# Slot reduction of the edge features by halving adds instead of a strided reduce, in a four-layer graph network on one core

## The chip, the core and the metric

The kernel runs on one core of a Trainium2 chip. The metric is device time in microseconds of one execution. The program is one launch; nothing else runs on the core. Its engines are named as in the profile: PE (TensorE), DVE (VectorE), ACT (ScalarE), POOL (GpSimd) and SP (SyncE, which here only issues DMAs).

## The reference

Four graph layers stand one behind the other, each with a residual and a layer norm, over 3125 nodes of 64 channels and 100,000 edges sorted by destination. The change is in the second layer, whose aggregation is this:

```python
xi = ew * m[dst]; xj = ew * m[src]; ea = ew * (edge_attr[:, :3] @ We + be)
h = jnp.concatenate([xi, xj, ea], axis=-1) @ Wpre + bpre
s1 = segment_sum(h, dst);  s2 = segment_sum(h * h, dst)
mn = segment_min(h, dst);  mx = segment_max(h, dst)
```

So for each node and each channel four values are folded over the node's incoming edges: the sum of h, the sum of its squares, the largest and the smallest h.

## The kernel before

Nodes are ordered by their number of edges and cut into 25 blocks of 128, one node per partition. A block is worked off in steps. In one step every node of the block takes up to 16 of its edges (16 slots); the step's word in `step_word` holds how many of the 16 slots are in use. There are 62 steps, and they need 815 slots together. The first layer runs over these steps in LOOP0, the second in LOOP1. The later layers use other code here.

For every used slot POOL issues one indirect DMA (line 544, called in line 630's loop) that gathers 128 rows of `b_tab` into the slot's place in the buffer G1[u], 64 floats per partition; u is 0 and 1 in turn, so that the gathers of one step run beside the work on the step before it. POOL may start a step's gathers when its row numbers have been loaded by SP (`lin<-lin_tab`) and when DVE has read the buffer two steps ago (`LOOP1.free`).

DVE, in `step1`, waits for the gathered rows; adds the block's own term (line 1674); waits for the edge's attributes and multiplies by the edge weight (1678); counts relations (1679 to 1684); waits for PE's product of the edge attributes (line 817) and adds it from PSUM (1686). Now h of this step stands in `hh[u][:, :, 0:64]`, 16 slots by 64 channels. ACT squares it into `hh[u][:, :, 64:128]` (1046) and makes masked copies `hmax[u]` and `hmin[u]`, 16 slots by 64 channels each, with 32 small instructions (1049); then it makes the next step's `eaT` (1043), which PE waits for. In the first 50 steps (25 pairs) DVE also builds one-hot tiles for a histogram on PE (1514, 1515), and in the even ones of these it splits packed counts (1692 to 1694) that ACT unpacks (1034 to 1036).

The last thing that DVE does in a step is `add_step` (lines 1656 to 1668), on the buffers of the step before: ACT has had a step's time to fill them. It folds the 16 slots of `hh`, `hmax` and `hmin` to one, and folds the results into the block's accumulators `accS`, `accMx` and `accMn`. After the loop one more `add_step` takes the last step. `add_step` runs 63 times (62 in the loop, the first on a neutral fill). All the order on an engine is the order in which the code is written; between engines semaphores are waited for. `d()` is a drain of DVE, put between an instruction and one that reads its result.

LOOP0 has a similar fold: lines 1559 and 1563 halve a tile of 16 slots by 68 with adds, and line 1553, a product of two tiles in SBUF, stands ahead of it.

Of the kernel before, what the change touches and what calls it, by code (L numbers as in the profile page):

```python
# [27 lines left out]
ALU = mybir.AluOpType  # L28
ACT = mybir.ActivationFunctionType
X_AXIS = mybir.AxisListType.X  # L30

P = 128
N, E, C, R = 3125, 100000, 64, 9
# [27 lines left out]
def build(nc, a, out):  # L61
# [18 lines left out]
    with ExitStack() as ctx:  # L80
        sb = lambda name, shape, dt=F32: ctx.enter_context(nc.sbuf_tensor(name, shape, dt))
# [5 lines left out]
        def at(off, parts, *shape, dt=F32):  # L87
            n = 1
            for s in shape:
                n *= s  # L90
            v = arena[0:parts, off:off + n]
            if dt != F32:
                v = v.bitcast(dt)
            if len(shape) == 2:
                v = v.rearrange("p (a b) -> p a b", b=shape[1])
            if len(shape) == 3:
                v = v.rearrange("p (a b c) -> p a b c", b=shape[1], c=shape[2])
            return v
# [36 lines left out]
        accMx = at(14100, P, NB, C)  # L135
        accMn = at(15700, P, NB, C)
        accS = at(17300, P, NB, 2 * C)
        accS1, accS2 = accS[:, :, 0:C], accS[:, :, C:]

        hh = [at(4160 + 4240 * u, P, SLOTS, 2 * C) for u in range(2)]  # L140
        hmax = [at(6352 + 4240 * u, P, SLOTS, C) for u in range(2)]
        hmin = [at(7376 + 4240 * u, P, SLOTS, C) for u in range(2)]
# [42 lines left out]
        WeR = sb("WeR", [C, SLOTS, 3])  # L185
        score = [sb(f"score{u}", [P, SLOTS, HEADS]) for u in range(2)]
        expd = [sb(f"expd{u}", [P, SLOTS, HEADS]) for u in range(2)]
        red = sb("red", [P, 4 * C])
        rel_hot = sb("rel_hot", [P, SLOTS, R])
        rel_sum = sb("rel_sum", [P, R])  # L190
        relF = sb("relF", [P, R])
# [914 lines left out]
        def _(dve):  # L1106
            ring = {"mm": 0, "q": 0, "stage": 0}
            tt, ts, stt, red_ = dve.tensor_tensor, dve.tensor_scalar, dve.scalar_tensor_tensor, dve.tensor_reduce
            d = dve.drain
# [133 lines left out]
            for pair in PAIRS:  # L1243
                s = ring["stage"] % NSTAGE
                if ring["stage"] >= NSTAGE:
                    dve.wait_ge(stage_out[s], 16 * (ring["stage"] // NSTAGE))
                n = len(pair)
# [362 lines left out]
            for g in GROUPS:  # L1610
                n = len(g)
# [17 lines left out]
            for g in GROUPS:  # L1629
                n = P * len(g)  # L1630
                mm_take(lambda bank: dve.tensor_copy(T1[0:C, g[0] * P:g[0] * P + n], bank[0:C, 0:n]))
            for pair in PAIRS:
                k = ring["mm"]
                dve.wait_ge(mm_full, k + 1)
                s = slice(pair[0], pair[-1] + 1)
# [20 lines left out]
            def add_step(g, u):  # L1656

                blk = block_in(before)
                parts = ((hh[u], accS, ALU.add, red[:, 0:2 * C]), (hmax[u], accMx, ALU.max, red[:, 2 * C:3 * C]),
                         (hmin[u], accMn, ALU.min, red[:, 3 * C:4 * C]))  # L1660
                dve.wait_ge(hmin_ready, g + 1)
                for t, acc, op, r in parts:
                    red_(r, t.rearrange("p s c -> p c s"), X_AXIS, op)  # L1663
                d()
                for t, acc, op, r in parts:
                    v_ = acc[:, bass.ds(blk, 1), :]
                    tt(v_, v_, r.unsqueeze(1), op)
                d()

            def step1(i, u, with_hist):  # L1670
                blk = block_in(word[u])
                h = hh[u][:, :, 0:C]
                wait_rows(LOOP1, u)
                tt(h, G1[u], aR[:, bass.ds(blk, 1), :].to_broadcast([P, SLOTS, C]), ALU.add).then_inc(index_used, 1)  # L1674
                dve.wait_ge(attrs_in[u], 16 * (i + 1))
                prepare_step(2 * i + u + 1, 1 - u)
                d().then_inc(LOOP1.free, 1)
                tt(h, h, bc(ewm[u], C), ALU.mult)
                tt(rel_hot[:], bc(relation[u], R), bm(relF[:], SLOTS), ALU.is_equal)
                d()  # L1680
                red_(rel_sum[:], rel_hot[:].rearrange("p s r -> p r s"), X_AXIS, ALU.add)
                d()
                v_ = accT[:, bass.ds(blk, 1), :]
                tt(v_, v_, rel_sum[:].unsqueeze(1), ALU.add)
                dve.wait_ge(edge_terms, 2 * i + u + 1)
                tt(h, h, mm[:].rearrange("p a (s c) -> p (a s) c", c=C), ALU.add).then_inc(h_ready, 1)  # L1686
                if with_hist:
                    type_hots(1, 2 * i + u + 2 * HI, 8 * (2 * i + u) + 16 * HI, u)
                if with_hist and u == 0:
                    dve.wait_ge(pack_in, 16 * (i + 1))  # L1690
                    dve.wait_ge(pack_cast, i + 1)
                    ts(even_sb, pack_sb, 0x070707, None, op0=ALU.bitwise_and)
                    ts(odd_sb, pack_sb, 3, 0x071F1F, op0=ALU.logical_shift_right, op1=ALU.bitwise_and)
                    ts(top_sb, pack_sb[:, 0:P], 22, 3, op0=ALU.logical_shift_right, op1=ALU.bitwise_and)
                    d().then_inc(pack_split, 1)
                add_step(2 * i + u, 1 - u)
                end_step(u)
# [4 lines left out]
            with dve.Fori(HI, pairs) as i:  # L1702
                for u in range(2):
                    step1(i, u, False)
            d()
            add_step(2 * pairs, 1)
            dve.wait_ge(pack_cast, NB + 1)
            red_(totF[:, 0:1], edge_sums[:].rearrange("p k b -> p (k b)"), X_AXIS, ALU.add)
# [31 lines left out]
            for g in GROUPS:  # L1740
                k = ring["mm"]
                dve.wait_ge(mm_full, k + 1)
                s = slice(g[0], g[-1] + 1)
# [7 lines left out]
            for pair in PAIRS:  # L1751
                n = len(pair)
# [83 lines left out]
            for g in GROUPS:  # L1836
                n = len(g)
# [18 lines left out]
            for lo, hi, b in ((lo, hi, b) for lo, hi in PARTS for b in range(lo, hi)):  # L1856
# [10 lines left out]
                if b == hi - 1:  # L1867
                    v_ = sumL3[:, lo:hi]
# [32 lines left out]
```

## Time and profile before

| | us |
|---|---|
| median of 3 runs | 3041.29 |
| lowest, highest | 3036.68, 3044.48 |
| the profiled execution's own time | 3036.68 |
| its span in the profile | 3035.0 |
| LOOP1, first gather to last | 1423.7 to 2495.4 |
| DVE's work on LOOP1, to the last accumulate | to 2521.4 |

| engine | busy us | share of the span |
|---|---|---|
| DVE | 2074.2 | 68% |
| POOL | 1797.3 | 59% |
| PE | 1456.4 | 48% |
| ACT | 1191.8 | 39% |

The profile is of one execution. Times in it count from the start of the span. An engine's busy share is a mean over stages with other limits, so that what sets the time of LOOP1 has to be read from the waits there, not from this table.

### The profile page before, as it was taken

Reading aid. Unit: us, or ns where it says so; the run is one execution under the profiler, and the core shown is the slowest. Engines: PE = TensorE matmul, PEld = TensorE weight load, DVE = VectorE, ACT = ScalarE, POOL = GpSimd, SP = SyncE. Lnnn points to the kernel's source line nnn. Section 1 sums busy time; section 2 is a strip of 40 time slices with the busy share of each in tenths; the row PEclk is TensorE's granted clock in tenths of the full one; section 3 lists DMA queues with packets and bytes.
Section 4 is the critical chain, followed back from the end, with each engine's and each line's share of the span. In section 5 each row is a group of like instructions: output and inputs, shape, how many; then the busy total and the mean of one; then the engine's idle time right before and its main releaser. Section 6 shows DMA issues by size and latency. Waiting matters only on the chain.

```text
span 3035.0 us, 29175 instructions
## 1 busy us (share of the span) xinstructions
PE 1456.4 (48%) x4543; PEld 629.0 (21%) x4544; DVE 2074.2 (68%) x3745; ACT 1191.8 (39%) x3184; POOL 1797.3 (59%) x1818
## 2 busy tenths in 40 slices
PE   2125555656545443443444444443443233497975
PEld 1101111212111111121111111111111003474542
DVE  6846777777756666666778888886777786513176
ACT  0013333434334334430556666664555553010121
POOL 3457777777777777721777777677777760000213
PEclk7556666666665566666555555555555556598965
DMA  5232222222222222210222222222222110163200
GB/s 136 53 75 57 57 62 58 58 58 56 60 60 61 58 62 62 63 31 23 57 57 58 68 60 58 62 59 57 57 58 43 30 27 2 54 270 130 87 1 11
DMA packets 124335, 186.48 MB, mean 61 GB/s; under 512 B 62046, under 2 KB 79155, under 8 KB 124128
## 3 DMA queue, kind: packets, MB, share of 16 engines
q0 software_dynamic: 57776, 89.59, 14.6%
q1 hardware_dynamic: 48894, 70.70, 7.2%
q10 hardware_dynamic: 17618, 25.71, 2.4%
q8 instruction: 13, 0.21, 0.0%
q14 instruction: 34, 0.27, 0.0%
HBM read 146.04 MB, written 39.84 MB: 61 GB/s over the span
## 4 chain that ended last, share of the span: by engine, by line
POOL 15%; PE 14%; issue 11%; DVE 10%; ACT 6%; DVEq 2%; DMA 2%; POOLq 2%; ACTq 0%; SPq 0%
POOL arena L544 15%; PE mm L683 3%; ACT arena L1049 3%; PE l L878 3%; DVE red L1663 3%; PE mm L817 2%; PE l L904 1%; PE tp L667 1%; PE mm L878 1%; PE hist L878 1%; PE mm L904 1%; DMA arena<-kv_tab,rec 1%; POOLq L630 1%; DVE arena L1686 1%; POOLq L624 1%
## 5 line engine op out<-in xcount | busy, mean ns | idle before, releaser
L544 POOL DMA_INDIRECT arena<-b_tab,lin x815 | 809.3, 993 | 367.8 <-issue 247.5
L544 POOL DMA_INDIRECT arena<-kv_tab,rec x815 | 817.3, 1003 | 254.7 <-issue 238.3
L737 PE MATMUL l<-arena,identB 128*128 128x512 bf16 x996 | 400.5, 570 | 527.6 <-DVE arena L1544 518.0
L1049 ACT ACTIVATE arena<-arena,lin 128x64 f32<-128x64 f32 x1984 | 479.6, 333 | 0.0
L1663 DVE TENSOR_REDUCE red<-arena 128x128 f32<-128x2048 f32 x189 | 459.5, 2486 | 13.6 <-issue 12.8
L817 PE MATMUL mm<-Wslots,eaT 48*128 48x512 f32 x248 | 234.2, 1097 | 399.7 <-ACT eaT L1043 390.2
L1544 DVE TENSOR_SCALAR arena<-arena,digit 128x512 bf16<-128x512 int16 x744 | 257.4, 415 | 57.0 <-PE l L737 43.0
L759 PE MATMUL hist<-arena,oh_lo 125*128 125x225 bf16 x400 | 170.6, 584 | 244.5 <-DVE arena L1515 244.5
L737 PEld LDWEIGHTS l<-arena,identB 128*128 128x128 bf16 x996 | 115.9, 128 | 801.1 <-DVE arena L1544 621.3
L544 POOL DMA_INDIRECT arena<-cnt_tab,infoR x25 | 26.7, 1068 | 373.8 <-DVEq L1834 366.5
L1046 ACT ACTIVATE arena<-arena 128x1024 f32<-128x1024 f32 x62 | 65.6, 1057 | 447.2 <-DVE arena L1686 447.2
L996 ACT ACT_TABLE_LOAD x31 | 39.8, 1283 | 416.6 <-DVEq L1539 416.6
L1005 ACT ACTIVATE arena<-T,digit,negdigit 128x512 bf16<-128x512 f32 x248 | 188.4, 806 | 8.6
L1674 DVE TENSOR_TENSOR arena<-arena 128x1024 f32<-128x1024 f32 x62 | 76.0, 1226 | 153.2 <-DMA arena<-b_tab,lin 135.2
L817 PEld LDWEIGHTS mm<-Wslots,eaT 48*128 48x128 f32 x248 | 72.2, 321 | 490.6 <-ACT eaT L1043 416.2
L759 PE MATMUL hist<-T,oh_lo 125*128 125x225 bf16 x400 | 169.8, 581 | 4.9 <-DVE T L1515 4.5
L1521 DVE TENSOR_TENSOR arena<-arena 128x1024 f32<-128x1024 f32 x62 | 76.0, 1226 | 137.2 <-DMA arena<-kv_tab,rec 136.1
L1002 ACT ACTIVATE T<-arena,negcode 128x512 f32<-128x512 int16 x248 | 164.5, 710 | 4.3
L759 PEld LDWEIGHTS hist<-arena,oh_lo 125*128 125x128 bf16 x400 | 53.9, 148 | 398.5 <-DVE arena L1515 323.1
L996 ACT ACTIVATE expd<-score 128x64 f32<-128x64 f32 x62 | 15.9, 256 | 304.3 <-DVEq L1539 304.0
L878 PE MATMUL l<-arena 128*128 128x192 bf16 (+1 forms) x750 | 98.2, 295 | 57.9 <-DVEq L1810 39.2
L918 ACT ACTIVATE T<-tp 64x512 f32<-64x512 f32 (+3 forms) x49 | 25.3, 543 | 238.5 <-PE tp L667 238.3
(381 smaller groups left out, 2515.6 us busy)
## 6 DMA issues: line engine op xcount, KB each, us to landing
arena<-at_tab SPq DMA_DIRECT2D x50, 800.0 KB, 5.8
at_tab<-T ACTq DMA_DIRECT2D x25, 800.0 KB, 3.4
arena<-kv_tab,rec POOLq DMA_INDIRECT x815
arena<-b_tab,lin POOLq DMA_INDIRECT x815
at_pack<-arena SPq DMA_DIRECT2D x25, 256.0 KB, 2.1
T<-at_pack SPq DMA_DIRECT2D x25, 256.0 KB, 2.7
lin_tab<-lin ACTq DMA_DIRECT2D x62, 64.0 KB, 1.6
lin<-lin_tab SPq DMA_DIRECT2D x62, 56.0 KB
```

The lines of the kernel that those rows point to most:

```text
L544: return pool.indirect_dma_start(dst, None, table, offs(ap=index, axis=0))
L683: last = pe.matmul(mm[0:rows, k % 2, cols[0]:cols[1]], l, r, start=(t == 0), stop=(t == len(terms) - 1))
L737: last = pe.matmul(l3[:, 0, :], identB[:], hot[:, j], start=False, stop=True, skip_group_check=True)
L759: last = pe.matmul(hist[:, 0:NB * R], oh_lo[:, u, :, j], oh_hi[n][u][:, :, j], start=False, stop=True, skip_group_check=True)
L817: last = pe.matmul(mm[:, j, :], eaT[u], Wslots[:, 8 * j:8 * j + 8].rearrange("p s c -> p (s c)"), start=True, stop=True)
L878: last = pe.matmul(conv_banks[k][:, 0:w], atL[k][:, cols(t)], parts[:, t].rearrange("p k c -> p (k c)"), start=(t == 0), stop=(t == NB - 1))
L1002: act.activation(distance[k], colI, ACT.Abs, bias=negcode[u][:, j + k:j + k + 1])
L1005: last = act.activation(onehotA[:, j + k], distance[k], ACT.Relu, scale=negdigit[u][:, j + k:j + k + 1], bias=digit[u][:, SLOTS - 4 + j + ...
L1049: last = act.activation(dst[:, s], hh[u][:, s, 0:C], ACT.Identity, bias=bias[:, s:s + 1])
L1521: tt(prod[:, :, 0:C], G[u][:, :, 0:C], q_, ALU.mult)
L1544: last = ts(onehot[:, (u + q) % 2, j], colI, G[u][:, s, 2 * C:2 * C + 1], digit[u][:, s:s + 1], op0=ALU.is_equal, op1=ALU.mult)
L1663: red_(r, t.rearrange("p s c -> p c s"), X_AXIS, op)
```

## The change

`add_step` folds the 16 slots in another way. Before, three `tensor_reduce` instructions each read a tile with the slot as the innermost index (a stride of 128 or 64 floats) and wrote one row of 128 or 64 floats into `red`. Now each tile is folded in place by four rounds of `tensor_tensor`: slots 0 to 7 with 8 to 15, then 0 to 3 with 4 to 7, and so on, with a drain behind each round. The accumulate reads slot 0 of the tile instead of `red`. `red` itself is smaller, since the largest that still uses it needs 2 x 64 floats.

```diff
-        red = sb("red", [P, 4 * C])
+        red = sb("red", [P, 2 * C + 4])
...
-                parts = ((hh[u], accS, ALU.add, red[:, 0:2 * C]), (hmax[u], accMx, ALU.max, red[:, 2 * C:3 * C]),
-                         (hmin[u], accMn, ALU.min, red[:, 3 * C:4 * C]))
+                folds = ((hh[u], accS, ALU.add), (hmax[u], accMx, ALU.max), (hmin[u], accMn, ALU.min))
                 dve.wait_ge(hmin_ready, g + 1)
-                for t, acc, op, r in parts:
-                    red_(r, t.rearrange("p s c -> p c s"), X_AXIS, op)
-                d()
-                for t, acc, op, r in parts:
+                for n in (8, 4, 2, 1):
+                    for t, acc, op in folds:
+                        tt(t[:, 0:n], t[:, 0:n], t[:, n:2 * n], op)
+                    d()
+                for t, acc, op in folds:
                     v_ = acc[:, bass.ds(blk, 1), :]
-                    tt(v_, v_, r.unsqueeze(1), op)
+                    tt(v_, v_, t[:, 0:1], op)
                 d()
```

The first place is DVE's stream in the first step of a pair with the histogram, at the end of the step. Line 1694 is the last instruction ahead of `add_step`, `ISA` rows are drains and register work. Before:

```order
L1694 TENSOR_SCALAR arena<-T1 128x128
L1437 ISA x2
L1663 TENSOR_REDUCE red<-arena 128x128
L1663 TENSOR_REDUCE red<-arena 128x64 x2
L1667 ISA
L1667 TENSOR_TENSOR arena<-arena,red 128x128
```

Now:

```order
L1694 TENSOR_SCALAR arena<-T1 128x128
L1437 ISA x2
L1663 TENSOR_TENSOR arena<-arena 128x1024
L1663 TENSOR_TENSOR arena<-arena 128x512 x3
L1663 TENSOR_TENSOR arena<-arena 128x256 x3
L1663 TENSOR_TENSOR arena<-arena 128x128 x3
L1663 TENSOR_TENSOR arena<-arena 128x64 x2
L1667 ISA
L1667 TENSOR_TENSOR arena<-arena 128x128
```

Three instructions have become twelve, at the same place and behind the same wait; a row such as `128x512 x3` joins the last two of one round and the first of the next. What follows, the three accumulates, is as before.

The second place is the `add_step` behind the loop, on DVE; `L1702` is the branch that closes the loop and line 1708 the first instruction of what comes after. Before:

```order
L1702 COMPARE_AND_BRANCH
L1437 ISA x2
L1661 ISA
L1663 TENSOR_REDUCE red<-arena 128x128
L1663 TENSOR_REDUCE red<-arena 128x64 x2
L1667 ISA
```

Now:

```order
L1702 COMPARE_AND_BRANCH
L1437 ISA x2
L1660 ISA
L1663 TENSOR_TENSOR arena<-arena 128x1024
L1663 TENSOR_TENSOR arena<-arena 128x512 x3
L1663 TENSOR_TENSOR arena<-arena 128x256 x3
L1663 TENSOR_TENSOR arena<-arena 128x128 x3
L1663 TENSOR_TENSOR arena<-arena 128x64 x2
L1667 ISA
```

Nothing else moves on DVE, and the streams of POOL, ACT, PE and SP are the same.

## Rows read from the trace of the kernel before

**Rows 1.** Page, part 1: busy us, share of the span, instructions.
```profile
PE 1456.4 (48%) x4543; PEld 629.0 (21%) x4544; DVE 2074.2 (68%) x3745; ACT 1191.8 (39%) x3184; POOL 1797.3 (59%) x1818
```

**Rows 2.** Chain of waits in LOOP1, 1440 to 2525 us, shares by line.
```profile
by line: POOL arena L544 37.3%; issue 22.4%; ACT arena L1049 9.2%; DVE red L1663 7.2%; PE mm L817 4.5%; POOLq L630 1.7%; DVE arena L1686 1.6%; POOLq L624 1.6%; ACT arena L1046 1.4%; ACT T L1034 1.4%; ACT T L1035 1.4%; DVE arena L1678 1.2%; 
```

**Rows 3.** Groups, POOL in LOOP1: busy us, mean ns | idle before, releasers.
```profile
L544 POOL DMA_INDIRECT arena<-b_tab,lin x815 | 809.3, 993 | 367.8 <-issue 247.5 <-DVEq L1471 105.4 <-DMA lin<-lin_tab 14.9
```

**Rows 4.** Line 544, LOOP1: ns min/median/max; a wait of it, a wait for it (us, times).
```profile
L544 POOL DMA_INDIRECT arena<-b_tab,lin x815: 938/944/1877, 1423.7 to 2494.5; - x163
...
  DMA lin<-lin_tab: 14.9, 6
...
  DVE arena L1674: 136.3, 41
```

**Rows 5.** Groups, DVE in LOOP1, shapes apart.
```profile
L1663 DVE TENSOR_REDUCE red<-arena 128x128 f32<-128x2048 f32 x63 | 233.5, 3706 | 13.6 <-issue 12.8 <-ACT arena L1049 0.9
L1663 DVE TENSOR_REDUCE red<-arena 128x64 f32<-128x1024 f32 x126 | 231.2, 1876 | 0.0
...
L1667 DVE TENSOR_TENSOR arena<-arena,red 128x64 f32 x126 | 22.6, 221 | 0.0
...
L1667 DVE TENSOR_TENSOR arena<-arena,red 128x128 f32 x63 | 18.4, 292 | 11.5 <-issue 11.5
```

**Rows 6.** Groups, DVE in LOOP0, shapes apart, 300 to 1300 us.
```profile
L1553 DVE TENSOR_TENSOR arena<-arena 128x1024 f32<-128x1024 f32 x53 | 65.0, 1226 | 3.9
...
L1559 DVE TENSOR_TENSOR arena<-arena 128x544 f32<-128x544 f32 x54 | 39.2, 726 | 6.4
```

**Rows 7.** Timeline, LOOP0: start us, us, engine, line [idle before].
```profile
1197.81 1.23 DVE L1553 TENSOR_TENSOR arena<-arena 128x1024 f32<-128x1024 f32 x1
1198.72 1.13 POOL L544 DMA_INDIRECT arena<-kv_tab,rec  x1 [0.30 <-issue]
1199.15 1.25 DVE L1559 TENSOR_TENSOR arena<-arena 128x544 f32<-128x544 f32 x2
1200.15 1.06 POOL L544 DMA_INDIRECT arena<-kv_tab,rec  x1 [0.30 <-DMA rec<-rec_tab,win]
```

**Rows 8.** Timeline, LOOP1, a step without the histogram.
```profile
2349.82 7.20 DVE L1663 TENSOR_REDUCE red<-arena 128x128 f32<-128x2048 f32 x3
...
2350.06 0.94 POOL L544 DMA_INDIRECT arena<-b_tab,lin  x1 [0.30 <-issue]
...
2357.22 0.59 DVE L1667 TENSOR_TENSOR arena<-arena,red 128x128 f32 x3 [0.19 <-issue]
```

**Rows 9.** Timeline, LOOP1, an even step with the histogram, then an odd one.
```profile
2298.94 7.30 DVE L1663 TENSOR_REDUCE red<-arena 128x128 f32<-128x2048 f32 x3 [0.51 <-issue]
2299.07 0.94 POOL L544 DMA_INDIRECT arena<-b_tab,lin  x1 [0.30 <-issue]
...
2314.39 0.68 DVE L1514 TENSOR_TENSOR oh_lo<-arena,hist_part 125x1024 bf16<-125x1024 bf16 x1
...
2314.62 1.26 POOL L544 DMA_INDIRECT arena<-b_tab,lin  x1 [0.30 <-issue]
2314.99 1.09 DVE L1515 TENSOR_TENSOR arena<-arena,hist_code 125x1800 bf16<-125x1800 bf16 x1
...
2315.99 7.35 DVE L1663 TENSOR_REDUCE red<-arena 128x128 f32<-128x2048 f32 x3
2316.19 0.94 POOL L544 DMA_INDIRECT arena<-b_tab,lin  x1 [0.30 <-issue]
```

**Rows 10.** Timeline, LOOP1, where DVE sets the pace.
```profile
2003.47 1.23 DVE L1674 TENSOR_TENSOR arena<-arena 128x1024 f32<-128x1024 f32 x1 [0.68 <-issue]
...
2036.83 1.23 DVE L1674 TENSOR_TENSOR arena<-arena 128x1024 f32<-128x1024 f32 x1 [0.68 <-issue]
```

**Rows 11.** Timeline, the end of LOOP1.
```profile
2489.53 1.22 DVE L1686 TENSOR_TENSOR arena<-arena,mm 128x1024 f32<-128x1024 f32 x1
...
2503.50 1.22 DVE L1686 TENSOR_TENSOR arena<-arena,mm 128x1024 f32<-128x1024 f32 x1 [0.43 <-PE mm L817]
```

## The prediction, on record before the changed kernel ran

> **What bounds the kernel now.** I read the busy shares first, then the chain of waits of LOOP1 alone, then POOL's and DVE's groups there, then the timeline of single steps. DVE is the busiest engine of the kernel [rows 1], which makes a shorter fold on DVE look like a gain. The chain of waits in LOOP1 says otherwise: 37.3% of it is POOL's gather and 22.4% "issue", the 0.30 us between two gathers; the reduce has 7.2% [rows 2]. POOL confirms it. Its 815 gathers are busy for 809.3 us [rows 3], and the idle time inside the run of gathers is 247.5 us of issue [rows 3] and 14.9 us in 6 waits for row numbers [rows 4]. 809.3 + 247.5 + 14.9 = 1071.7, which is the whole stretch from the first gather to the end of the last (1423.7 to 2495.4). So LOOP1 is as long as POOL's gathers make it, but for 13.1 us (14.9 less 6 x 0.3 that it would have spent anyway), and DVE waited 41 times, 136.3 us in all, for gathered rows [rows 4]. DVE sets the pace only in a middle stretch, where line 1674 starts 0.68 us behind the step before it without waiting for rows, and two steps take 33.36 us [rows 10].
>
> The second thing to see is what lengthens a gather. Its median is 944 ns and its mean 993 [rows 3, 4]: 815 x 0.944 = 769.4, so 39.9 us are excess. The excess is not spread; it sits on gathers that start while DVE runs an instruction with two inputs in SBUF. In LOOP0 line 1553 ends at 1197.81 + 1.23 = 1199.04, and the gather that started inside it ends at 1199.85; the two halving adds of line 1559 end at 1200.40, and the gather that started in the second ends at 1201.21 [rows 7]. Both end 0.81 us behind the end of the instruction that they met. In LOOP1 the gather at 2314.62 met line 1514, which ends at 2315.07, and ends at 2315.88: again 0.81 [rows 9]. Three rules come from these. A gather that meets such an instruction ends 0.81 us behind its end (never under 0.94 in all). It is held by the one it met, not by the next: line 1515 followed without a pause and did not hold it. And the reduce of line 1663 holds nobody: gathers at 2350.06, 2299.07 and 2316.19 started inside it and took 0.94 [rows 8, 9].
>
> The Trainium skill ("SBUF — State Buffer", section "SBUF: two separate sides") states that VectorE and GpSimd share one pair of ports, that a VectorE instruction with two SBUF inputs takes it for its whole length, and that the other engine then fully blocks. The rows above agree in that direction. The same section has the lock work both ways, so that a gather would hold DVE out for its own length; the rows disagree there, since line 1515 ran at once and for 1.09 us beside the gather that had just been let in. By the two-way rule each round of the tree could be pushed back by part of a gather, which DVE's slack in this loop would absorb where it waits for rows.
>
> **The change part by part.** *DVE's own time.* For contiguous adds, 1024 elements take 1226 ns and 544 take 726 [rows 6]: 1.042 ns an element and 159 ns. So 693 ns for 512, 426 for 256, 292 for 128 (which the accumulate also shows [rows 5]) and 226 for 64. Without a drain between them neighbours overlap: the accumulates take 0.292 + 2 x 0.221 = 0.734 one by one, and three together some 0.56 to 0.59 [rows 5, 8], so I take 0.087 off each. With a drain the next starts some 0.075 late (3.9 us of idle in 53 times behind a drain [rows 6]). The rounds are then 2.44, 1.37, 0.84 and 0.57 us, with three gaps 5.44. The reduces take 3.706 + 2 x 1.876 less two overlaps of 0.065 = 7.33, as the rows of 7.20 to 7.35 show [rows 5, 8, 9]. DVE saves some 1.8 us 63 times, 113 us. Nearly all of it lies beside POOL's gathers and turns into a longer wait at line 1674. No bound on DVE's side can alter that: were the tree free, POOL would still need its 1058 us.
>
> *POOL's gathers under the tree.* For 5.44 us of every step, DVE now runs two-input adds nearly without a gap, and the trace tells where the gathers stand against them. Relative to the tree's start the instructions end at 1.23, 1.83, 2.44, then 3.21, 3.55, 3.89, then 4.39, 4.59, 4.80, then 5.17, 5.31, 5.45. Without the histogram a gather starts 0.24 in (2350.06 against 2349.82 [rows 8]). It meets the first add and ends at 2.04, after 1.80 us: 0.86 more. The next starts at 2.35, meets the third, and would end at 3.25, where 3.29 is its normal end: nothing. The next starts at 3.60, meets the sixth, ends at 4.70: 0.16 more. The next starts at 5.01, meets the tenth, ends at 5.98: 0.03. Together 1.05 us. In an even step with the histogram the first gather is 0.13 in [rows 9]: 0.97 more, then the same: 1.15. In an odd one it is 0.20 in (2316.19 against 2315.99): 0.90 more, 1.09. These places hold from step to step, since the gather ahead was itself released at the end of a DVE instruction. 61 of the 63 folds run beside gathers: 11 x 1.05 + 25 x 1.15 + 25 x 1.09 = 67.6 us.
>
> The trace shows no tree in LOOP1, so I bound this. Over all places of the gathers against the tree the same working gives from 0.14 (first gather 0.05 ahead of the first add's end) to 1.34 us (just inside it), mean 0.74. Over 61 folds that is 9 to 82 us, mean 45. I take 67.6, from the places that the rows show; below nothing is not excluded by the rule alone, and is a rival.
>
> *What goes.* POOL's 13.1 us of waits: they arise in the middle stretch, where POOL had run two buffers ahead of DVE. With the fold on POOL the steps of 12 and 13 gathers there take 12.5 x 1.25 + 0.6 + 1.1 = 17.3 us on POOL, and DVE needs 16.68 - 1.8 = 14.9, so POOL no longer waits. In the same stretch line 1674 itself fell on gathers, up to the longest of 1.88 us [rows 4]; there are nine such and nine smaller ones, some 10 us, of which some 6 go when DVE waits for rows again.
>
> *The end.* Line 1686 repeats every 13.97 us there (2489.53 to 2503.50), waiting for PE [rows 11], which waits for ACT's 33 instructions of the step before; no DVE time is in that chain. Its last step stands closer behind POOL now, some 2 us, since POOL's last steps of 10 gathers come to 13.6 us. The last fold waits 0.9 for ACT [rows 5], is bare behind it and saves 1.8. Together 4.
>
> *The rest.* Three more drains per fold are in the 5.44. No wait is added. The smaller `red` shifts later tiles by 496 bytes, which changes no shape or order: nothing, within 2 us either way.
>
> Sum: 67.6 - 13.1 - 6 - 4 = +44. On the profiled execution's own 3036.7 (span 3035.0 and 1.7 around it) this gives 3081. The median of the three runs is 4.6 above that execution, their lowest, so a new median may lie anywhere up to 5 above the sum; the range takes that in.
>
> **The rivals.** *The gathers drift over all places.* Landing times vary, and a gather may fall elsewhere in the tree. Then 45 - 13.1 - 6 - 4 = +22: 3059. For it: some gathers behind line 1674 do scatter. Against: rows 8 and 9, a first gather at 0.13, 0.20 and 0.24.
>
> *No collision.* Short adds with drains between them might let each gather through. The place is POOL's queue, the price nothing, and what is left is -13.1 - 4 = -17: 3020, faster. It decides at what a collision costs on average: under 17 / 61 = 0.28 us a fold the change gains. For it: most gathers behind the first lose little by my own working. Against: line 1559 held a gather with an add of 0.44 us [rows 7], and the tree's first add is 1.23 us long, as line 1553. The Trainium skill ("Advanced Engine Details and Errata", section "VectorE Performance Modes") notes that GpSimd is disturbed by VectorE's two-port modes, which a float add of two tensors does not use; taken alone that would give this rival's 3020. Rows 7 and 9 speak against it.
>
> *DVE sets the pace.* If LOOP1 were DVE's, 1.8 us x 62 = 112 us would go. Only the stretch around 2003 to 2037 is DVE's [rows 10], and the two steps of 33.36 us there could fall to 2 x 13.97 + 3.9 (ACT's unpack) = 31.9 at most, some 20 us over 27 steps; but POOL's own time allows only the 13.1 above. This ends with the last rival at 3020.
>
> *Worst place.* Every first gather just inside the first add: 82 - 23 = +59: 3096.
>
> **How the numbers follow.** Forecast 0.60 (its own range 3065 to 3095), drift 0.22, worst place and beyond 0.08, no collision or DVE's pace 0.10. The range of 3050 to 3105 leaves out the faster rivals and little above. About 0.3%, 9 us, is what a measurement of this kernel can tell from no change: faster 0.08, same 0.06, slower 0.86.
>
> **What would show it.** Right: line 1663 sums to some 5.3 us busy per fold; line 544 in LOOP1 has its median still at 0.94 but a mean near 1.05 and some 100 us of excess, with one gather of 1.8 to 1.9 us at the head of each tree; DVE's wait for rows at line 1674 grows by some 2.5 us a step; POOL's waits for `lin` are gone; everything before 1424 us is as it was. Wrong: gathers inside the tree at 0.94, or adds of line 1663 that are longer than those of line 1559 at the same size, or PE's or ACT's chain setting the steps before the last ones.

## The result, and the profile after

| | before | changed |
|---|---|---|
| median, us (4 runs each, same chip) | 3042.89 | 3085.46 |
| lowest to highest | 3036.68 to 3049.04 | 3084.12 to 3089.38 |
| profiled execution's own time, span | 3036.68, 3035.0 | 3082.18, 3080.5 |
| gathers of LOOP1, first start to last end | 1423.7 to 2495.4 | 1424.5 to 2545.3 |

The ratio is 1.0142, 95% interval 1.0119 to 1.0166: the changed kernel is slower by 1.4%. In the medians that is 42.6 us, in the profiled spans 45.5. The profiled execution of the changed kernel (3082.18) is a further one, not among the four.

The page's first part shows why busy shares mislead here. DVE is busy 133 us less than before [rows 1], and POOL 59 us more:

```profile
PE 1451.5 (47%) x4536; PEld 634.2 (21%) x4544; DVE 1941.3 (63%) x4312; ACT 1191.3 (39%) x3184; POOL 1856.0 (60%) x1818
```

The chain of waits in LOOP1 (here 1440 to 2570 us) has lost nearly all that was not POOL; the gather has gone from 37.3% to 57.8% and issue from 22.4% to 32.8% [rows 2]:

```profile
by line: POOL arena L544 57.8%; issue 32.8%; POOLq L630 2.6%; POOLq L624 2.3%; ACT arena L1049 1.3%; DMA arena<-b_tab,lin 0.5%; POOLq L622 0.3%; DVE arena L1663 0.3%; PE mm L817 0.3%; DVE arena L1686 0.2%; ACT arena L1046 0.2%; DMA lin<-lin
```

The group of POOL's gathers, and the view of line 544 with its waits, answer to [rows 3] and [rows 4]. The gathers are as many; their median is still 0.945 us, but the mean is 1.068 instead of 0.993. The 14.9 us of waits for `lin` are gone, and DVE now waits 309.4 us for rows (136.3 before):

```profile
L544 POOL DMA_INDIRECT arena<-b_tab,lin x815 | 870.1, 1068 | 358.6 <-issue 250.7 <-DVEq L1471 107.9
```

```profile
L544 POOL DMA_INDIRECT arena<-b_tab,lin x815: 938/945/1983, 1424.5 to 2544.4; - x163
...
  DVE arena L1674: 309.4, 56
```

DVE's groups in LOOP1, by shape (busy us, mean ns, idle before). The five rows of line 1663 sum to 347.4 us, 5.51 a fold before overlaps; the two rows of [rows 5] sum to 464.7, 7.38 a fold:

```profile
L1663 DVE TENSOR_TENSOR arena<-arena 128x512 f32<-128x512 f32 x189 | 124.7, 688 | 4.7
L1663 DVE TENSOR_TENSOR arena<-arena 128x1024 f32<-128x1024 f32 x63 | 77.0, 1222 | 15.5 <-issue 12.8 <-ACT arena L1049 2.7
...
L1663 DVE TENSOR_TENSOR arena<-arena 128x256 f32<-128x256 f32 x189 | 74.3, 421 | 4.7
...
L1663 DVE TENSOR_TENSOR arena<-arena 128x128 f32<-128x128 f32 x189 | 49.1, 287 | 4.7
...
L1663 DVE TENSOR_TENSOR arena<-arena 128x64 f32<-128x64 f32 x126 | 22.3, 219 | 0.0
```

The timeline of one fold of the changed kernel, in the same kind of step as [rows 8]. The fold starts at 2389.61. The gather 0.23 us behind its start takes 1.80 us and ends at 2391.64, which is 0.81 behind the end of the first add (2389.61 + 1.22). Of the three behind it one is free, one takes 1.08 and one 0.97:

```profile
2389.61 5.40 DVE L1663 TENSOR_TENSOR arena<-arena 128x1024 f32<-128x1024 f32 x12
...
2389.84 1.80 POOL L544 DMA_INDIRECT arena<-b_tab,lin  x1 [0.30 <-issue]
2391.95 0.95 POOL L544 DMA_INDIRECT arena<-b_tab,lin  x1 [0.30 <-issue]
2393.20 1.08 POOL L544 DMA_INDIRECT arena<-b_tab,lin  x1 [0.30 <-issue]
2394.59 0.97 POOL L544 DMA_INDIRECT arena<-b_tab,lin  x1 [0.30 <-issue]
```

And an odd step with the histogram, to set against the last rows of [rows 9]:

```profile
2355.07 5.40 DVE L1663 TENSOR_TENSOR arena<-arena 128x1024 f32<-128x1024 f32 x12
...
2355.27 1.84 POOL L544 DMA_INDIRECT arena<-b_tab,lin  x1 [0.30 <-issue]
2357.42 0.94 POOL L544 DMA_INDIRECT arena<-b_tab,lin  x1 [0.31 <-issue]
2358.67 1.09 POOL L544 DMA_INDIRECT arena<-b_tab,lin  x1 [0.30 <-issue]
2360.06 0.96 POOL L544 DMA_INDIRECT arena<-b_tab,lin  x1 [0.30 <-issue]
```

### The profile page after: what moved, and what is told of

The parts are those of the page before. It is cut to its first block, busy times and chain, and to the rows that moved or that the text cites. A ratio compares the mean times of both kernels' runs of the same rounds, so it can differ in the third digit from the quotient of the medians.

```text
span 3080.5 us, 29924 instructions
## 1 busy us (share of the span) xinstructions
PE 1451.5 (47%) x4536; PEld 634.2 (21%) x4544; DVE 1941.3 (63%) x4312; ACT 1191.3 (39%) x3184; POOL 1856.0 (60%) x1818
## 4 chain that ended last, share of the span: by engine, by line
POOL 23%; issue 15%; PE 13%; DVE 5%; POOLq 2%; ACT 2%; DMA 1%; DVEq 1%; ACTq 0%
POOL arena L544 23%; PE mm L683 4%; PE l L878 3%; PE l L904 1%; PE tp L667 1%; PE mm L878 1%; PE hist L878 1%; POOLq L630 1%; POOLq L624 1%; PE mm L904 1%; DMA arena<-kv_tab,rec 1%; ACT arena L1049 0%; DMA rec<-rec_tab,win 0%; PE hist L904 0%; PE l L737 0%
## 5 line engine op out<-in xcount | busy, mean ns | idle before, releaser
L544 POOL DMA_INDIRECT arena<-b_tab,lin x815 | 870.1, 1068 | 358.6 <-issue 250.7
L737 PE MATMUL l<-arena,identB 128*128 128x512 bf16 x990 | 388.5, 557 | 530.8 <-DVE arena L1544 518.5
L1663 DVE TENSOR_TENSOR arena<-arena 128x1024 f32<-128x1024 f32 x756 | 326.3, 487 | 29.6 <-issue 12.8
L1674 DVE TENSOR_TENSOR arena<-arena 128x1024 f32<-128x1024 f32 x62 | 76.7, 1236 | 314.3 <-DMA arena<-b_tab,lin 309.4
L1521 DVE TENSOR_TENSOR arena<-arena 128x1024 f32<-128x1024 f32 x62 | 76.0, 1226 | 135.0 <-DMA arena<-kv_tab,rec 133.8
```

The costliest lines, as they stand in the source:

```text
L544: return pool.indirect_dma_start(dst, None, table, offs(ap=index, axis=0))
L737: last = pe.matmul(l3[:, 0, :], identB[:], hot[:, j], start=False, stop=True, skip_group_check=True)
L1663: tt(t[:, 0:n], t[:, 0:n], t[:, n:2 * n], op)
```

## The experiments

The kernel before ran beside each of them on the same chip. The first four (e1 to e4) shared its runs, and so did the next four and the last three; these three groups were on three chips, so that kernels of different groups are best compared by their ratios. "Excess" is the gathers' busy time in LOOP1 over 815 x 0.944 = 769.4 us.

| kernel | median us | ratio to before (95%) | gathers busy, LOOP1 | excess | POOL's waits for `lin` |
|---|---|---|---|---|---|
| before | 3038.8 to 3043.7 | | 809.3 | 39.9 | 14.9 |
| changed | 3085.5 | 1.0142 (1.0119 to 1.0166) | 870.1 | 100.7 | 0 |
| e1, PSUM input | 3027.9 | 0.9953 (0.9936 to 0.9970) | 811.4 | 42.0 | 0 |
| e2, pieces of 128 | 3117.5 | 1.0254 (1.0237 to 1.0272) | 897.2 | 127.8 | 1.5 |
| e3, only hh by adds | 3075.6 | 1.0118 (1.0098 to 1.0138) | 857.6 | 88.2 | 2.4 |
| e4, `red` wide | 3087.9 | 1.0154 (1.0133 to 1.0175) | 868.3 | 98.9 | 0 |
| e5, pieces of 512 | 3054.8 | 1.0037 (1.0024 to 1.0049) | 838.3 | 68.9 | 0 |
| e6, pieces of 256 | 3043.2 | 1.0006 (0.9996 to 1.0015) | 825.7 | 56.3 | 2.1 |
| e7, only the head with PSUM | 3057.5 | 1.0042 (1.0027 to 1.0057) | 839.3 | 69.9 | 0.3 |
| e8, other lines cut | 3064.8 | 1.0065 (1.0049 to 1.0082) | 790.0 | 20.6 | 37.6 |
| e9, pieces of 128 with pauses | 3058.0 | 1.0053 (1.0038 to 1.0068) | 829.4 | 60.0 | 11.0 |
| e10, all of LOOP1 cut | 3044.3 | 1.0009 (1.0001 to 1.0018) | 819.3 | 49.9 | 9.5 |
| e11, and LOOP0's | 3039.5 | 1.0000 (0.9992 to 1.0009) | 819.6 | 50.2 | 10.1 |

### e1: the same adds, second input in PSUM

```diff
-                        tt(t[:, 0:n], t[:, 0:n], t[:, n:2 * n], op)
+                        tt(t[:, 0:n], t[:, 0:n], bm(l3[:, 0, 0:t.shape[2]], n), op)
```

> The twelve adds of the changed fold stay, with the same sizes, order and drains, but their second input is one row in PSUM repeated over the slots instead of the other half of the tile (so the sums are not those of the reference). Theory (a gather on POOL is held by a DVE instruction with two inputs in SBUF): nothing in the fold holds a gather any more, the mean gather of LOOP1 is back at or under 0.993 us, POOL's run of gathers is some 60 us shorter than with the changed kernel, and the time is 3020 to 3035, below the kernel before. Rival A (the loop got longer by DVE's extra instructions and drains, or by traffic of the adds in SBUF): the adds still write the same tiles and are as many, so the time stays near 3085. Rival B (phase only, any DVE instruction holds gathers): mean gather stays near 1.07 us.

The theory held, but for 3 ns in the mean gather (996, where at most 993 was expected): POOL's run of gathers is 60.5 us shorter than with the changed kernel, and the time is in the range. The group of gathers and one fold of this kernel:

```profile
L544 POOL DMA_INDIRECT arena<-b_tab,lin x815 | 811.4, 996 | 357.2 <-issue 248.9 <-DVEq L1471 108.3
```

```profile
2339.66 5.35 DVE L1663 TENSOR_TENSOR arena<-arena,l 128x1024 f32<-128x1024 f32 x12
...
2339.90 0.94 POOL L544 DMA_INDIRECT arena<-b_tab,lin  x1 [0.30 <-issue]
2341.15 0.94 POOL L544 DMA_INDIRECT arena<-b_tab,lin  x1 [0.30 <-issue]
2342.39 0.94 POOL L544 DMA_INDIRECT arena<-b_tab,lin  x1 [0.30 <-issue]
```

DVE's fold takes 5.35 us against 5.40, so its work is the same, instructions, drains and writes to SBUF included, and no gather is held. That takes 57.6 us off the changed kernel. It also shows the size of what the change was able to give: 10.9 us under the kernel before by the medians, 14 by the ratio, where the prediction had put 17 for no collision.

The new second input is also one row repeated over the slots, so the repetition could be what frees the gathers. The kernel before excludes it. Lines 1674 and 1678 have a repeated second input in SBUF, and in LOOP1 85 gathers that started in them took 0.97 us and more; line 1686 has a second input in PSUM that is not repeated, and none of the 51 gathers that started in it was lengthened.

Two inputs in SBUF are enough to hold a gather, but not the only way. In the kernel before, line 1692, a bitwise AND of integers with one input and its output in SBUF, lengthened each of the 25 gathers that started in it, to some 1.04 us, again to 0.81 behind its end. The strided reduce, which has one input too, lengthened none of 353. What separates the two was not tested.

```profile
2297.53 0.42 DVE L1692 TENSOR_SCALAR T<-T 128x512 int32<-128x512 int32 x1
...
2297.73 1.04 POOL L544 DMA_INDIRECT arena<-b_tab,lin  x1 [0.30 <-issue]
```

### e7: only the head of the fold with PSUM

```diff
-                        tt(t[:, 0:n], t[:, 0:n], t[:, n:2 * n], op)
+                        head = n == 8 and t is hh[u]
+                        tt(t[:, 0:n], t[:, 0:n], bm(l3[:, 0, 0:2 * C], n) if head else t[:, n:2 * n], op)
```

> The changed fold, with only its first instruction (1024 elements of hh) reading its second input from one repeated row in PSUM instead of slots 8 to 15, so that the sums are not those of the reference; the other eleven adds as in the changed kernel. Theory: the first gather of a fold is no longer held (0.94 instead of 1.80 to 1.91 us). The next starts at 1.38 to 1.49 and meets the second add (end 1.83), losing 0.2 to 0.3; the next loses 0.13; the rest nothing. Loss of the fold 0.4 instead of 1.08: 42 us less than the changed kernel, 3037 to 3050. Rival (the loss follows the time spent in adds with two inputs in SBUF, 1.2 of 5.4 us gone): a fifth of the loss goes, some 3070.

The first gather is free, as expected, and 30.8 us of excess go; the time is 8 us above the expectation. The gathers that follow now stand elsewhere:

```profile
2382.90 1.21 DVE L1664 TENSOR_TENSOR arena<-arena,l 128x1024 f32<-128x1024 f32 x1
2383.14 0.94 POOL L544 DMA_INDIRECT arena<-b_tab,lin  x1 [0.30 <-issue]
2384.03 4.13 DVE L1664 TENSOR_TENSOR arena<-arena 128x512 f32<-128x512 f32 x10
2384.39 1.14 POOL L544 DMA_INDIRECT arena<-b_tab,lin  x1 [0.30 <-issue]
2385.83 1.07 POOL L544 DMA_INDIRECT arena<-b_tab,lin  x1 [0.30 <-issue]
2387.21 1.06 POOL L544 DMA_INDIRECT arena<-b_tab,lin  x1 [0.30 <-issue]
```

Here 0.20, 0.13 and 0.12 us are lost where I had allowed for the first two, and in steps with the histogram the second gather took 1.25. Neither a fifth of the loss (the rival) nor all that I expected: a gather that is set free moves all behind it. Taking the head away takes half of the fold's cost, not 0.9 of it: what the gathers lose inside the folds, summed over LOOP1, is 62.6 us in the changed kernel and some 32 here, with 3 more beside the accumulates behind them.

### e3: only hh folded by adds

```diff
+                for n in (8, 4, 2, 1):
+                    tt(hh[u][:, 0:n], hh[u][:, 0:n], hh[u][:, n:2 * n], ALU.add)
+                    d()
+                for k, (t, acc, op) in enumerate(folds[1:]):
+                    red_(red[:, k * C:(k + 1) * C], t.rearrange("p s c -> p c s"), X_AXIS, op)
```

> Half of the change: hh (2048 elements) is folded by the four rounds of adds, hmax and hmin by the strided reduce as before. Theory: what costs is the head of the fold, the add of 1024 elements that the first gather of the fold meets 0.13 to 0.24 us after its start (0.9 to 0.97 of the 1.08 us). It is still there, so most of the loss stays: some 0.9 x 61 = 55 us of added excess, less the 13 us of POOL's waits if DVE (which saves some 1 us a fold) no longer holds it up: 3070 to 3085. Rival C (loss goes by the time in adds): 1920 of 3840 elements remain, half of the loss: about 3062. Rival A (instruction count): 4 + 2 instead of 12, a third of the loss: about 3050.

3075.6, inside the theory's range; the rivals had 3062 and 3050. Half the elements and a third of the instructions leave 48.3 of the 60.8 us of added excess: the head is still there.

### e4: `red` at its old width

```diff
-        red = sb("red", [P, 2 * C + 4])
+        red = sb("red", [P, 4 * C])
```

> The changed kernel with red at its old width of 256 floats, so that all later tiles stand at their old addresses. Theory: no effect, 3080 to 3090. Rival (the shift of later tiles by 496 bytes costs or gains something): a difference from the changed kernel of more than 9 us.

3087.9, two runs: within 3 us of the changed kernel, and the intervals of the two ratios overlap. The shift of later tiles has no effect that can be measured.

### e5, e6 and e2: the adds of the changed fold in pieces of 512, 256 and 128

```diff
-                        tt(t[:, 0:n], t[:, 0:n], t[:, n:2 * n], op)
+                        k = max(1, 512 // t.shape[2])          # 256, 128
+                        for s in range(0, n, k):
+                            e = min(s + k, n)
+                            tt(t[:, s:e], t[:, s:e], t[:, n + s:n + e], op)
```

The first of these to run was the one with pieces of 128. Its expectation speaks of 39 adds a fold; the trace shows 31.

> The changed fold, each add of over 128 elements cut into pieces of 128 (39 adds a fold instead of 12, same elements, same drains, result unchanged). Theory (a gather ends 0.81 us behind the end of the one DVE instruction that it met, and is free behind it): a piece takes 0.29 us, so a gather that meets one loses at most 0.16 us; five gathers per fold lose some 0.3 us together instead of 1.08, POOL's excess falls by some 45 us to 55, although DVE is busy some 1.3 us longer per fold. Time 3035 to 3050, about the kernel before. Rival A (more instructions cost): 27 more per fold x 61 x 0.072 us is 119 us more of DVE, time above 3085. Rival C (the share of time that DVE spends in such adds sets the loss, whatever their length): the loss grows a little, 3085 to 3100.

A clear miss of the theory, and in the region of Rival A (more instructions cost): 3117.5, the slowest of all. The timeline of one fold shows three gathers that lose 0.13 us, as the theory has it, and one that takes 2.52:

```profile
2410.40 6.71 DVE L1666 TENSOR_TENSOR arena<-arena 128x128 f32<-128x128 f32 x31
...
2410.64 1.07 POOL L544 DMA_INDIRECT arena<-b_tab,lin  x1 [0.30 <-issue]
2412.01 2.52 POOL L544 DMA_INDIRECT arena<-b_tab,lin  x1 [0.30 <-issue]
2414.83 1.08 POOL L544 DMA_INDIRECT arena<-b_tab,lin  x1 [0.30 <-issue]
2416.21 1.07 POOL L544 DMA_INDIRECT arena<-b_tab,lin  x1 [0.30 <-issue]
```

It ends at 2414.53, so it was let in at 2413.72, 3.32 us into the fold. That is where the first round of 16 pieces ends. 44 gathers of LOOP1 took over 1.95 us (none in the kernel before, two in the changed one), and 42 of them were held in this way to the end of a first round. So the rule "ends 0.81 us behind the instruction that it met" is not the whole of it, and the next kernels tested its limit.

> The changed fold with its one add of 1024 elements cut into two of 512; nothing else. The pieces of 128 had left some gathers held not to the end of the piece that they met but to the end of the whole round (2.52 to 2.93 us in all). Theory 1 (a gather is released at the end of the instruction it met): the first gather of a fold, 0.13 to 0.24 us in, now ends at 0.69 + 0.81 = 1.50, taking 1.26 to 1.37 instead of 1.80 to 1.91; the second starts at 1.81 and ends free or nearly; the fold's loss falls from 1.08 to some 0.65 us, 26 us less over the loop: 3055 to 3065. Theory 2 (in a round of four or more adds without a pause a later gather waits for the round's end): the second gather, from 1.81, is held to 2.52 + 0.81 = 3.33, 1.52 us: the loss is some 1.2 us, 3085 to 3100. Rival (instruction count): one more per fold, 0.07 us on DVE, no change from 3085.

> The changed fold with adds of over 256 elements cut into pieces of 256 (18 adds, 8 of them in the first round, 4 in the second). Theory 1 (released at the end of the piece met): a gather loses at most 0.3 us, a fold some 0.5 us: 3045 to 3060. Theory 2 (a later gather waits for the end of its round): the second gather of the fold, from 1.2 to 1.5 us in, is held to the end of the first round at 2.8 and ends at 3.6, 2.1 to 2.4 us in all: loss of the fold 1.4 to 1.7 us, 3100 to 3120.

Both came out as theory 1 has it, at or a little under the lower ends of its ranges: 3054.8 (0.2 under) and 3043.2 (1.8 under). The same stretch with pieces of 512, then of 256:

```profile
2380.49 5.51 DVE L1666 TENSOR_TENSOR arena<-arena 128x512 f32<-128x512 f32 x13
2380.73 1.26 POOL L544 DMA_INDIRECT arena<-b_tab,lin  x1 [0.30 <-issue]
```

```profile
2371.02 5.88 DVE L1666 TENSOR_TENSOR arena<-arena 128x256 f32<-128x256 f32 x18
...
2371.26 1.00 POOL L544 DMA_INDIRECT arena<-b_tab,lin  x1 [0.30 <-issue]
2372.56 1.03 POOL L544 DMA_INDIRECT arena<-b_tab,lin  x1 [0.30 <-issue]
```

The gather 0.24 us into the fold takes 1.80, 1.26 and 1.00 us as the add that it meets has 1024, 512 and 256 elements, while DVE's fold grows from 5.40 to 5.51 and 5.88 us. That excludes that the instruction count or the share of time in such adds is what costs, Rival A of the pieces of 128 included. With pieces of 256 the whole loss of the change is gone: the gathers still lose 21.7 us inside the folds, but that is offset by the waits for `lin` that went and the shorter end.

### e9: pieces of 128, with a drain behind every fourth of the first round

```diff
+                            if n == 8 and done and done % 4 == 0:
+                                d()
                             tt(t[:, s:e], t[:, s:e], t[:, n + s:n + e], op)
+                            done += 1
```

> The kernel of pieces of 128, with a drain behind every fourth piece of the first round (three drains more a fold). There, a gather that started 0.16 us behind the start of a piece (1.20, 1.41 or 1.61 us into the fold) was held until 3.33, the end of the first round of 16 pieces, and took 2.5 to 2.9 us; one that started 0.20 behind a piece's start was free. Theory (such a gather is passed over at every seam between pieces and gets in at the first pause of DVE): the pauses end after 0.9, 1.95 and 3.0 us of the round, so it is held for 0.9 us at most, no gather of a fold takes over 1.9 us, and the excess falls from 130 us to 60 to 90: 3050 to 3085. Rival (the hold has a length of its own, or ends with the round for another reason): gathers of 2.5 us and more stay, near 3117 or above.

The time came out in the theory's range, with an excess of 60.0 us at its lower end, and the ratio to the kernel before falls from 1.0254 to 1.0053 by three more drains in a fold. No gather that starts inside a fold takes over 1.12 us. The longest of LOOP1, 1.86 us, stands beside a histogram line, which was not changed:

```profile
1755.85 1.09 DVE L1515 TENSOR_TENSOR arena<-arena,hist_code 125x1800 bf16<-125x1800 bf16 x1
...
1755.90 1.86 POOL L544 DMA_INDIRECT arena<-b_tab,lin  x1 [0.30 <-issue]
```

So breaking up the unbroken run of pieces ends the long holds. How it does so is only in part shown. The drains also shift the pieces: the gather that starts 1.41 us into the fold, which stood 0.19 behind a piece's start in the kernel of pieces of 128, now stands 0.03 behind one. In the first round of e9 no gather stood where the held ones had stood, so the run does not show what such a gather would do at a drain. In the second round, which has eight pieces and no drain inside, 46 gathers started 0.19 to 0.20 us behind the start of the seventh piece; all of them were passed over at the next seam and ended 0.81 us behind the end of the round (1.11 us). That agrees with a gather that gets in at a pause of DVE, but there the pause is only one piece away.

Why a gather is passed over is open, and the expectation's reading of the phase does not stand. The pieces start 0.202 us apart, so that the gathers at 1.20, 1.41 and 1.61 started 0.19 behind a piece's start, not 0.16. In the kernel of pieces of 128, 41 gathers that started 0.186 to 0.199 us behind a piece's start (the fold's first piece left out) were held to the end of the first round, and 36 that started 0.190 to 0.199 behind one went free. The phase does not tell the two apart.

### e8: the kernel before, with its other long adds and products cut

```diff
-                tt(h, h, bc(ewm[u], C), ALU.mult)
+                for s in range(0, SLOTS, 4):
+                    tt(h[:, s:s + 4], h[:, s:s + 4], bc(ewm[u][:, s:s + 4], C), ALU.mult)
...                                    # 1674, 1521 and 1553 likewise, 1514, 1515 and 1559 in two, three and more
```

> The kernel before, its fold untouched, with the other long DVE instructions of two SBUF inputs cut: lines 1521, 1553, 1674 and 1678 into four pieces of 4 slots, 1514 into two, 1515 into three, 1559 into pieces of two slots. These hold gathers for some 40 us in LOOP1 and 40 in LOOP0. Theory 1 (released at the end of the piece met): most of the excess goes in both loops, 3041 less 30 to 50: 2990 to 3015. Theory 2 (a gather can be held to the end of an unbroken run of pieces): the runs are as long as the uncut instructions or longer, so the excess stays or grows a little and DVE's extra 0.9 us a step adds where DVE sets the pace: 3035 to 3070.

In LOOP1 theory 1 held for the gathers (excess 39.9 to 20.6) and was wrong about the time, which lies in theory 2's range, though not by theory 2's longer holds: the longest gather of LOOP1 takes 1.25 us. POOL's waits for `lin` grew from 14.9 to 37.6 us and gave the saving back, so that its run of gathers is as long as before (1071.1 against 1071.7 us). That DVE had no room for the added instructions where it sets the pace is the likely reason:

```profile
L544 POOL DMA_INDIRECT arena<-b_tab,lin x815 | 790.0, 969 | 396.6 <-issue 243.4 <-DVEq L1471 115.5 <-DMA lin<-lin_tab 37.6
```

The whole loss stands ahead of LOOP1, whose first gather stands at 1449.8 instead of 1423.7, 26 us later. Which of the cuts in LOOP0 did that was not tested apart; e11, with fewer of them, does not have it (1419.6).

### e10 and e11: cuts where DVE has room again

The diff of e10 is that of e6 and, in LOOP1 alone, the cuts of e8; e11 has in LOOP0 also line 1553 in four pieces and the 544 of line 1559 in two.

> The changed fold in pieces of 256, and in LOOP1 also lines 1674 and 1678 in four pieces of 256, 1514 in two and 1515 in three; LOOP0 as before. The pieces in the fold cost POOL some 17 us; cutting the other lines took 19 us of excess away in LOOP1 but made DVE slower, and POOL waited 37.6 us for it; the fold by adds gives DVE 1.4 us a step back. Theory: excess 30 to 40 us, no waits of POOL, POOL's run of gathers 1050 to 1060 us instead of 1071.7, the last step 2 us closer: 3020 to 3032, faster than both kernels. Rival (phases of the gathers move and give it back): 3035 to 3050.

> The same, and in LOOP0 line 1553 in four pieces and the adds of 544 of line 1559 in two. Those two lines hold gathers for some 31 us in LOOP0. Theory: half of it or more goes, 10 to 20 us under the one without: 3005 to 3020. Rival (LOOP0 is held by DVE in stretches, and four more instructions of 0.07 us a step come back as waits, as where 1521 and the one-hot lines were cut as well and LOOP0 grew by 26 us): 3025 to 3040.

Both theories were missed, e10's by 12 us, e11's by 20, and both times lie in the range of the rival. Neither kernel beats the one before.

Against e6, whose fold is the same, the gathers lose 13.6 us less beside the other lines, which were cut (34.6 to 21.0). But inside the fold, whose instructions are as in e6, they lose 7.2 us more (21.7 to 28.9): the first gather of a fold starts 0.68 us in at the median, where it was 0.20, and the ones behind it meet other pieces. And 7.4 us of waits for `lin` came back (2.1 to 9.5). That is the rival of e10, phases that move and give it back. In e11 the gathers of LOOP0 are busy 10.3 us less than in e10, and 3.0 us of that reached LOOP1's start. No kernel that computes the reference was found to be faster than the one before.

## Why the prediction was right

**What bounds the kernel.** Right: LOOP1 grew by what POOL's run of gathers grew, 1071.7 to 1120.8 us (49.1), while DVE did 133 us less.

**DVE's fold.** 5.44 us predicted, 5.40 measured, against 7.30 before. Over 63 folds that saves 119 us; the prediction wrote 113, because it rounded its own 7.33 - 5.44 = 1.89 down to 1.8. The saving turned into DVE's wait for rows: it grew by 173 us (136.3 to 309.4), which is the 119 saved and the 49 by which POOL's run grew, within 5 us. That is 2.8 us a step against the 2.5 predicted.

**Gathers under the fold.** The positions and lengths worked out from the rows came out to the second digit: 1.80, nothing, 1.10, 0.97 predicted without the histogram, 1.80, 0.95, 1.08, 0.97 measured; 1.84, 1.10, 0.97 in the odd step, 1.84, 1.09, 0.96 measured. Of the 61 folds beside gathers, 56 have them at the predicted places (first gather 0.13 to 0.24 us in). They could be read from the trace of before because gathers ahead of a fold are themselves released at a DVE instruction's end, so that phases are renewed in each step.

The places were taken from single steps, though, and the trace of before does not bear them out throughout. In the middle stretch, where DVE sets the pace, the first gather of a fold started 1.20 us in and not 0.20 in 11 of the 25 odd steps with the histogram, as here:

```profile
1611.28 7.35 DVE L1663 TENSOR_REDUCE red<-arena 128x128 f32<-128x2048 f32 x3
...
1612.48 0.94 POOL L544 DMA_INDIRECT arena<-b_tab,lin  x1 [0.30 <-issue]
```

In the changed kernel nine of these eleven stand at 0.20, since DVE waits for rows again; the prediction did not say so. Five folds, between 1947 and 2030 us, have the first gather at 0.98 to 1.20 and lose 0.26 to 0.75 us instead of 1.1.

**The size, in part by luck.** With the collisions of line 1674 that go, +61.6 us were predicted (67.6 - 6) and +60.8 measured (870.1 less 809.3). Taken apart, both terms were off: inside the folds the gathers lost 62.6 us, 5.0 less than predicted, and beside all other lines they lost 1.8 less than before, where 6 had been put down. At line 1674 itself the loss fell from 14.4 to 11.2 us. That the two misses cancel is luck. That the fold's instructions are the cause is not: inside the folds nothing was lost before, 62.6 us with the change, and nothing in e1.

**What goes, and the end.** The waits for `lin` went, 14.9 us, of which 11.7 remain as a gain once the added issue of 3.2 is taken off (13.1 predicted). From the last gather's end to line 1708 it was 26.0 us and is 21.85: 4.2 less, 4 predicted. LOOP1's first gather starts 0.8 us later, which no term had.

The sum was +44; the profiled spans differ by 45.5 and the medians by 42.6. `red`'s width does nothing (e4). The runs also sized the rival without collisions (e1): the change would then gain 11 to 14 us, not 17.

Two things that were held are wrong, though they did not touch the number. That a gather is held by the one instruction that it met, and never by the next, is not so for unbroken runs of 128 (e2). It does hold where the pieces have 256 elements or more: in LOOP1 of the two kernels and of e1, e3, e5, e6 and e7, each gather of 0.965 us and more ended 0.81 to 0.83 us behind the end of the DVE instruction that had started last when it started. And the expectation of e3 had the head carry 0.9 of the cost: without it later gathers meet other adds, and half remains (e7).

On the Trainium skill ("SBUF — State Buffer", section "SBUF: two separate sides"): e1 agrees that it is the second input in SBUF that makes these adds hold a gather, since the same add with one in PSUM holds nobody (0.94 us). That the lock works both ways, the other engine shut out for the whole length, no run bears out: in e2 a piece beside which a gather got in took 0.32 to 0.35 us instead of 0.28, and not the gather's 0.94 longer. The rule that would have given the faster rival, two-port modes alone ("Advanced Engine Details and Errata", section "VectorE Performance Modes"), is refuted as the whole condition by the same pair of runs, the changed kernel and e1.

## What to carry to other kernels

Before making VectorE faster, find out which engine's run of work is as long as the loop; here it was GpSimd's indirect gathers, and a shorter fold with two SBUF inputs lengthened them by 61 us while saving 119 us of VectorE time that hardly anything waited for. Beside a stream of GpSimd gathers the price of such an instruction is set by its length where a gather meets it: a slow strided reduce cost them nothing, an add of 1024 elements at the head cost the gather that met it 0.86 to 0.97 us, a whole fold in pieces of 256 cost 0.36 us against 1.06, and an input in PSUM removes the cost. Do not take one input for safe: look for gathers beside each kind of instruction in your own trace. Where phases are locked, put each new instruction on the old timeline: here it gave the loss inside the folds as 67.6 us where 62.6 was measured. Look at more than one step per kind when you do so.

## What the runs showed of the hardware that was not expected

An unbroken run of short two-input adds can hold a gather for the whole run: with 16 adds of 0.28 us, one starting every 0.20 us without a drain between them, 42 gathers took 2.5 to 2.9 us (e2). With a drain behind every four, no gather inside a fold took over 1.12 us (e9). Gathers that started at the same phase of a piece, 0.19 to 0.20 us behind its start, were held in some folds and free in others; what decides it is open.

VectorE is held by gathers very little. With gathers held in every step the fold took 5.40 us, and 5.35 in the kernel where none was. In e2 a first round of 16 pieces lasted 3.30 to 3.33 us where a gather was held to its end and up to 3.45 where gathers got in between the pieces: letting one in cost the piece beside it 0.03 to 0.07 us.

A one-input instruction held gathers too: the bitwise AND of integers in line 1692, all 25 times, by 0.10 us each.
